# A graph layer's edge words sorted over four partitions at a time, for two batches at once, and 40 instead of 30 of 50 tiles read by one-hots

## The reference

```
h = relu(layernorm(x))
x = x + segment_sum((h * node_vec1)[src], dst) * node_vec1_n2
h = relu(layernorm(x))
x = x + (1 + eps) * h + segment_sum(relu(h[src] + edge_attr), dst)
```

## Time and profile before

| what | value |
|---|---|
| time, median of 3 runs (us) | 4988.89 (4985.14 to 4989.31) |
| the profiled execution's span (us) | 8580.9 |
| PE, DVE, ACT, POOL busy in it (us) | 4359, 3658, 3125, 3610 |
| indirect DMAs of POOL: scatters, gathers of layer two, gathers of middle tiles, of the last batch | 1875, 1250, 480, 50 |

### The profile page before, as it was taken

The page is one execution under the profiler, slowest core; times in us unless marked ns, Lnnn a source line. Parts: engine busy times, 40 slices in busy tenths (PEclk is TensorE's granted clock), DMA queues, the critical chain, the costliest instruction groups (busy, mean ns, idle before and its releaser), DMA issues.

```text
span 8580.9 us, 129759 instructions
## 1 busy us (share of the span) xinstructions
PE 4359.2 (51%) x44428; PEld 3164.9 (37%) x44428; DVE 3658.4 (43%) x11303; ACT 3124.7 (36%) x8299; POOL 3610.0 (42%) x3712
## 2 busy tenths in 40 slices
PE   0555555555555555555555555445444444545444
PEld 0333333333333333333333333334334343434343
DVE  6444444444444444444444444434343333434334
ACT  0333434343333333333333333234333333433333
POOL 7444444444444444444444444343443434343442
PEclk8777777777777777777777777666666666666666
DMA  5111111111111111111111100101110111101110
GB/s 90 31 31 31 31 31 31 31 30 31 30 31 30 31 30 31 30 31 30 31 30 31 31 17 17 43 22 31 30 32 22 32 29 32 31 22 32 30 32 17
DMA packets 437255, 265.45 MB, mean 31 GB/s; under 512 B 330740, under 2 KB 421220, under 8 KB 430120
## 3 DMA queue, kind: packets, MB, share of 16 engines
q1 hardware_dynamic: 318264, 185.91, 9.1%
q0 software_dynamic: 116960, 65.42, 4.4%
q10 hardware_dynamic: 1296, 4.79, 0.2%
HBM read 176.35 MB, written 79.52 MB: 30 GB/s over the span
## 4 chain that ended last, share of the span: by engine, by line
PE 36%; issue 26%; another core or an unknown queue 22%; DVE 9%; ACT 5%; SPq 1%; DVEq 0%; ACTq 0%; DMA 0%; POOL 0%; POOLq 0%
PE candidates L1179 16%; DVE arena L1663 5%; PE candidates L1105 5%; PE plain_ps L1191 4%; PE sorted_agg L1122 4%; DVE arena L1639 3%; PE key_rows L1074 2%; ACT centered L974 2%; PE candidates L1100 2%; ACT message L920 2%; PE plain_ps L1143 1%; PE candidates L1092 1%; ACT arena L821 1%; PE plain_ps L1151 1%
## 5 line engine op out<-in xcount | busy, mean ns | idle before, releaser
L710 POOL DMA_INDIRECT records<-stage,place_i x1875 | 1821.1, 971 | 675.8 <-issue 625.1
L698 POOL DMA_INDIRECT stage<-table,src_plain x1250 | 1193.9, 955 | 1778.1 <-DMA stage<-in_edge_attr 1386.7
L1639 DVE TENSOR_SCALAR arena<-arena,row_key 125x1280 bf16<-125x1280 f16 x1000 | 552.6, 553 | 2554.9 <-ACT arena L821 1776.0
L920 ACT ACTIVATE message<-candidates,member_is 128x96 bf16<-128x96 f32 x3600 | 912.4, 352 | 1643.5 <-remote 922.8
L691 POOL DMA_INDIRECT message<-table,mid_src x480 | 533.5, 1112 | 2234.8 <-PE plain_ps L1151 2095.5
L1105 PE MATMUL candidates<-parts,arena 125*128 125x32 bf16 x15000 | 589.2, 181 | 1214.2 <-issue 1211.8
L821 ACT ACTIVATE arena<-key_rows 125x640 f16<-125x640 f16 x1000 | 662.5, 719 | 1237.3 <-remote 987.2
L1663 DVE TENSOR_SCALAR arena<-window_iota,dst_rel 128x224 bf16<-128x224 f16 (+1 forms) x4800 | 1025.9, 280 | 112.4 <-remote 67.7
L1105 PEld LDWEIGHTS candidates<-parts,arena 125*128 125x128 bf16 x15000 | 503.7, 99 | 1384.6 <-issue 1370.1
L1092 PE MATMUL candidates<-parts,arena 125*128 125x96 bf16 x5000 | 312.0, 220 | 1312.9 <-ACT message L920 748.6
L1074 PE MATMUL key_rows<-ident,record 128*125 128x128 f16 x5000 | 494.6, 242 | 878.4 <-issue 587.7
(11 more groups left out here) (224 smaller groups left out, 5798.9 us busy)
## 6 DMA issues: line engine op xcount, KB each, us to landing
record<-records SPq DMA_DIRECT2D x50, 1650.0 KB, 7.1
stage<-in_edge_attr SPq DMA_DIRECT2D x125, 400.0 KB, 3.2
records<-pad SPq DMA_DIRECT2D x25, 1650.0 KB, 10.7
records<-stage,place_i POOLq DMA_INDIRECT x1875
stage<-table,src_plain POOLq DMA_INDIRECT x1250
message<-table,mid_src POOLq DMA_INDIRECT x480
xs<-in_x SPq DMA_DIRECT2D x8, 390.6 KB
table<-parts ACTq DMA_DIRECT2D x4, 585.9 KB
```

The source lines that it names most:

```text
L698: pool.indirect_dma_start(message[:, k, j, :] if l == 0 else rows[:, k, j, :], None, table0 if l == 0 else table1, bass.IndirectOffsetOnAx ...
L710: pool.indirect_dma_start(records, bass.IndirectOffsetOnAxis(ap=place_i[:, h, e:e + 1], axis=0), stage[:, h, e, :], None).then_inc(scatter ...
L920: last = nc.scalar.activation(direct_message[n % DB][:, m * WIDE:(m + 1) * WIDE], candidates[n % 2][:, m * WIDE:(m + 1) * WIDE], ACT.Copy, ...
L1639: nc.vector.tensor_scalar(src_onehot[:, g % 2, o, :], key_row[:, g % 2, :], row_key[0:NP, o:o + 1], None, ALU.is_equal).then_inc(src_oneho ...
```

## The change

The words of layer one are stored to DRAM once and come back as 64 rows of 200: four neighbouring partitions share a row (32 rows a batch), and two batches are sorted at the same time, in 25 rounds of MAX8 and MATCH_REPLACE8 over 200 words. Word 4k+j of the sorted row goes to tile k of the j-th of the four partitions, by a store to DRAM and a load. As 200 words are drawn instead of 50, a tile at a given rank meets fewer groups: the table `SPANS` gives 3 to 8. 20 tiles at either end are now read by one-hots, in eight steps of five instead of six, and 10 are gathered. The rounds of the sort stand in the main part of DVE's list, two to a group in groups 1 to 6 (12 rounds in an even batch, 13 and six closing passes in an odd one), the first pair's ahead of the first batch. SP issues the three transfers of a pair, ACT those of the first.

```diff
-    BOUNDS = (6, 7, 8, 8, 9, 9, 10, 10, 11, 11, 12, 12, 13, 13, 14)
-    SIDE = len(BOUNDS)
+    SPANS = ((0, 3), (0, 3), (0, 4), (0, 5), (0, 5), (0, 6), (0, 6), (0, 7), (1, 7), (1, 8),
+             (1, 8), (1, 9), (2, 9), (2, 10), (2, 10), (3, 10), (3, 11), (3, 11), (4, 12), (4, 12))
+    SIDE = 20
...
-        return range(BOUNDS[r]) if side == LOW else range(WIDES - BOUNDS[r], WIDES)
+        least, beyond = SPANS[r]
+        return range(least, beyond) if side == LOW else range(WIDES - beyond, WIDES - least)
...
+                if sorts_ahead(b) and h == 0:
+                    sp.wait_ge(words_out, 16 * (u + 1))
+                    sp.dma_start(pair_left, words_rows[bass.ds((b + 2) * QUADS, 2 * QUADS), :]).then_inc(pair_loaded, 16)
+                if sorts_ahead(b) and h == 1:
+                    sp.wait_ge(pair_steps, PAIR_STEPS * (u + 1))
+                    sp.dma_start(ordered_rows[bass.ds((b + 1) * QUADS, 2 * QUADS), :], pair_left).then_inc(words_out, 16)
+                    sp.wait_ge(words_out, 16 * (u + 2))
+                    sp.dma_start(row_words, ordered_v[:, bass.ds(b + 1, 2), :]).then_inc(words_loaded, 16)
...
+                if l == 0:
+                    act.wait_ge(direct_keyed, 1)
+                    act.dma_start(words_v, row_order[:]).then_inc(words_out, 16)
+                    act.wait_ge(words_out, 16)
+                    act.dma_start(pair_left, words_rows[0:2 * QUADS, :]).then_inc(pair_loaded, 16)
+                    act.wait_ge(pair_steps, PAIR_STEPS)
+                    act.dma_start(ordered_rows[0:2 * QUADS, :], pair_left).then_inc(words_out, 16)
+                    act.wait_ge(words_out, 32)
+                    act.dma_start(row_words, ordered_v[:, 0:2, :]).then_inc(words_loaded, 16)
...
+            def sort_pair(u, some):
...
+                for r in some:
+                    eight = pair_best[:, 8 * r:8 * r + 8]
+                    step(nc.vector.max(out=eight, in_=pair_left))
+                    if r < ROUNDS8 - 1:
+                        step(nc.vector.match_replace(out=pair_left, in_to_replace=eight, in_values=pair_left, imm_value=-1.0))
...
+                step(nc.vector.tensor_scalar(pair_left.rearrange("p (k e) -> p e k", k=SHARED), by_tile, pair_flag, None, ALU.add))
...
-            sort_rows(0, 0)
+            sort_pair(0, range(ROUNDS8))
+            dve.wait_ge(words_loaded, 16)
+            read_words(0, 0)
...
+                SORTING = [{g: range(2 * g - 2, 2 * g) for g in range(1, 7)}, {g: range(2 * g + 10, 2 * g + 12) for g in range(1, 7)}]
+                SORTING[1][7] = range(24, ROUNDS8)
...
                         if g == 4 and not is_first(b):
                             add_pair(b - 1)
+                        if sorts_ahead(b) and g in SORTING[h]:
+                            sort_pair(u, SORTING[h][g])
...
-                            sort_rows(b + 1, 1 - h)
...
+                            if s == SUBS - 4 and more:
+                                dve.wait_ge(words_loaded, 16 * (u + h))
+                                read_words(b + 1, 1 - h)
```

More of the change, by code:

```diff
@@ L80, in gnn_two_layers @@
     MID = PJ - DIRECTS
-    STEPS = ((LOW, range(4, -1, -1), "far"), (LOW, range(14, 9, -1), "arena"), (LOW, range(9, 4, -1), "near"),
-             (HIGH, range(14, 9, -1), "arena"), (HIGH, range(4, -1, -1), "far"), (HIGH, range(9, 4, -1), "near"))
-    SUBS = len(STEPS)
     SUB = 5
+    SIDE_STEPS = SIDE // SUB
+    SUBS = 2 * SIDE_STEPS
+    ROOMS = [("far", "arena", "near")[k % 3] for k in range(SUBS - 2)] + ["far", "near"]
+    STEPS = [(LOW, range(k * SUB, (k + 1) * SUB), ROOMS[k]) for k in range(SIDE_STEPS)]
+    STEPS += [(HIGH, range(SIDE - 1 - k * SUB, SIDE - 1 - (k + 1) * SUB, -1), ROOMS[SIDE_STEPS + k]) for k in range(SIDE_STEPS)]
+    LAST_ARENA = max(k for k in range(SUBS) if ROOMS[k] == "arena")
     TILE_OF = [(side, r) for side, ranks, _ in STEPS for r in ranks]
@@ L262, in gnn_two_layers @@
         wide_rooms += [record[0:NP, 1, :, :].rearrange("p t w -> p (t w)").bitcast(BF16)[:, w * SE5:(w + 1) * SE5] for w in range(IN_X)]
-        NEAR = BOUNDS[9]
-        assert NEAR + BOUNDS[4] <= len(wide_rooms)
+        NEAR = IN_X
+        assert all(len(STEP_GROUPS[k]) <= IN_X for k in range(SUBS) if ROOMS[k] != "arena")
         def wide_onehot(k, w):
@@ L288, in gnn_two_layers @@
         dst_far = sb("dst_far", [P, J], I32)
-        far = sb("far", [P, J])
-        far_dst = sb("far_dst", [P, J])
-        far_key = sb("far_key", [P, J])
+        far, far_dst, far_key = (row_room[:, (6 + k) * P:(6 + k) * P + J] for k in range(3))
         BANK = 512
@@ L368, in gnn_two_layers @@
         nodes_ready = sem("nodes_ready")
-        xs_steps = sem("xs_steps")
         result_ready = sem("result_ready")
@@ L495, in any_beyond, with sorts_ahead @@
             return eng.value_load(any_far_i[0:1, 0:1], min_val=0, max_val=1)
+        def sorts_ahead(b):
+            return not isinstance(b, int) or b < 2 + 2 * ROUNDS
         def is_last(b):
@@ L680, in _ @@
                       allow_small_or_imprecise_dtypes=True).then_inc(consts_ready, 1)
-            for r in range(SIDE):
-                pool.memset(bound[:, LOW, SIDE - 1 - r:SIDE - r], float(BOUNDS[r] * P)).then_inc(bounds_ready, 1)
-                pool.memset(bound[:, HIGH, r:r + 1], float((WIDES - BOUNDS[r]) * P)).then_inc(bounds_ready, 1)
+            GROUP_WORDS = P * LOWER
+            for q in range(PJ):
+                groups = met_by(HIGH, q) if q < SIDE else met_by(LOW, PJ - 1 - q) if q >= PJ - SIDE else range(WIDES)
+                pool.memset(least_word[:, q:q + 1], float(groups.start * GROUP_WORDS)).then_inc(bounds_ready, 1)
+                pool.memset(beyond_word[:, q:q + 1], float(groups.stop * GROUP_WORDS)).then_inc(bounds_ready, 1)
             pool.iota(members[:], pattern=[[1, MEMBERS]], base=0, channel_multiplier=0,
@@ L1706, in wide_onehots @@
                     dve.wait_ge(direct_copied_keys, SUBS * b + s + 1)
-                    if s == 1:
+                    held = [k for k in range(s) if ROOMS[k] == where]
+                    if held:
+                        dve.wait_ge(wide_picked, DIRECTS * b + FIRST[held[-1] + 1])
+                    elif where == "arena":
                         dve.wait_ge(sorted_done[0], GROUPS * (b + 1))
-                    elif s == 3:
-                        dve.wait_ge(wide_picked, DIRECTS * b + FIRST[2])
-                    elif s >= 4:
-                        dve.wait_ge(wide_picked, DIRECTS * b + FIRST[s - 3])
                     else:
```

138 lines of the change are left out of this document (82 added, 56 removed).

## The result

| | before | changed |
|---|---|---|
| time, median (us) | 4987.02 (4983.14 to 4989.31, 4 runs) | 5182.28 (5173.41 to 5202.59, 4 runs) |
| the profiled execution's span (us) | 8580.9 | 5171.3 |

The changed kernel is slower by 3.95%: a ratio of 1.0395, with a 95% interval of 1.0372 to 1.0418. Its recording is not stretched as that of before was: its span is that of a timed run (5171.3 of 5173.41 us), so stretches can be read from it directly.

What follows compares the result with a forecast made beforehand. POOL's DMAs bound the kernel before (125.6 us a batch); the changed PE/DVE/ACT loop, 117.1 - 1.1 + 14.5 = 130.5, replaces them. First middle products 260.5, batches 3233, then 52.5, 52.9, 55, 1652 and 61: 5105 us, range 4860 to 5300.

Steps and rivals of the forecast that it cites:

- What bounds before: Layer one: POOL's 95 DMAs bound a batch at 125.6 us; PE's loop with DVE and ACT takes 117.1, 8.5 to spare.
- What ten gathers fewer buy: POOL in 24 batches: 85 DMAs, 112.4 us a batch, 13.2 less; it buys only the distance to the next bound.
- The sort: DVE's main part: rounds of 1.10 us, groups of 5.3 instead of 3.12, all on the path: +14.5 us a batch.
- loop 117.1 - 1.1: PE's loop of 117.1 us a batch less 1.1 in the direct part: 116 in batches without a sort.
- 81.8 - 1.6 - 5.3: Direct part on PE: 81.8 us before, 1.6 of waiting in its last steps, net -5.3 of PE work by the change.
- 1652 + 61 of the sum: End of the kernel: layer two's 1250 gathers 1652 us, then 61 from the last gather to the end.
- The price of 1.322 us a DMA: POOL's indirect DMAs: 4608 us of the timed run for 3485 DMAs, if POOL is the bound throughout.
- The rule of the Trainium skill: POOL in busier main parts: lockout with DVE could make DMAs as slow as 1.54 us, 130.9 a batch.
- POOL stays the bound: Rival: PE and DVE's loop is below 125.5 us, change faster, 4820 at 10%; faster by either way 0.25.
- The loop is longer still: Rival: PE's loop before was near 125 us, sort on top, up to 5290, or 5370 with 2.02 us rounds; chance 0.19.
- The sort is hidden: Rival: DVE, idle for half of the span, hides the sort, giving 4800; faster by either way 0.25.
- the 5015 for a sort that does not grow: Rival case: sort time grows with no word, 11 us a pair-half instead of 14.5, giving 5015.

## Why the prediction held, and where it was off

The prediction (5105, within 4860 to 5300, slower) held: 5182.28 lies in the range, and slower is what it is. Of the 195 us that the change costs it had 116.

*What bounds before.* Right. POOL issues without a pause, 126.9 us a batch (125.6 in the prediction), and PE waits for records. The spare time of PE's loop, 8.5 us in the prediction, is 8.1 by the rows above. That the difference comes out is in part luck: both loops are longer than priced, POOL's by 1.3 us and the other (118.9 against 117.1) by 1.8.

*What ten gathers fewer buy.* Right in kind: the distance to the next bound, 183 us in the run that leaves only them out.

*The sort.* Right in place and size. Rounds of 1.08 us (1.10), 5.34 us a group (5.3), PE waiting for destination one-hots, and 135.06 - 120.8 = 14.3 us a batch where 14.5 was expected. The rival by which it is hidden in DVE's idle half fails for this placement; put into the direct part, the same rounds cost 121.8 - 120.8 = 1 us a batch.

*The mis-sized term* is "loop 117.1 - 1.1", the 116 us of a batch without the sort: 35.3 of main and 80.7 of direct part. It is 120.8. The two batches shown above of the run without the later sorts have 242.4 us where the prediction has 232, and the 10.4 lie in three places. The loop's jump, 3.5 us in the two, which the prediction did not have: in the kernel before it lies under PE's wait for POOL. The direct part, 1.0 longer in each: PE is busy for 76.2 us of it, where the prediction's prices leave 74.9 (81.8 - 1.6 - 5.3), a walk over tiles that left out small work on PE. And the main part, 2.5 longer in each even without the jump. That POOL scatters during it, which it did not do in the stretch that 35.3 was read from the earlier trace rows, is not the reason: in the kernel before with ten gathers fewer a main part with 28 scatters in it takes 34.25 us. That main part, its first matmuls up to the second set of picks, and the same 50 matmuls at the start of the main part of 37.80 us:

```profile
1950.79:1985.04 34.25, 27.72 (x418) 26.29 (x419) 31.15 (x115) 27.23 (x56) 26.02 (x28) 1.00 0.07 15
1950.79:1954.14 3.35, 3.35 (x50) 3.35 (x51) 3.09 (x14) 1.39 (x4) 2.44 (x4) 1.00 0.05 10
```

```profile
794.50 1.78 PE L1143 MATMUL candidates<-parts,arena 125*128 125x96 bf16 x20 [2.39 <-ACT message L971]
```

```profile
794.50:800.41 5.91, 5.91 (x50) 5.91 (x51) 5.54 (x22) 1.49 (x4) 4.58 (x5) 0.55 0.07 14
```

With a wait of 1.36 us for ACT ahead of them they ran at a granted clock of 1.00; with one of 2.39 us at 0.55, mostly the lower of its two levels (1.2 GHz), and took 2.56 us longer. That is most of the 3.55 us between these two main parts. The stretch of 35.3 us itself began slowly, behind a long wait (its first picks took 1.78 us, the 50 matmuls 5.16), so against it the start explains 0.75 of the 2.5; the rest stays open.

*Two errors that partly cancel.* Times 21 batches the loop was 96 us too short, and the first pick came at 187.4 instead of 180.6, mainly because the store of the words took 10.1 us instead of 4. Against that, layer two took 5171.3 - 3497.9 = 1673 us from its first gather, 40 less than the 1652 + 61 of the sum: 30 less up to the last gather and 10 less behind it. Together, 96 + 7 - 40 = 63 of the 65 us by which the 5171.3 of this execution lie above the 5106. The price of 1.322 us a DMA was one mean over both layers, where it is 1.34 in layer one of the kernel before (above) and 1622 / 1249 = 1.30 in layer two, by the line's own row in the changed kernel (durations in ns, first and last start):

```profile
L740 POOL DMA_INDIRECT stage<-table,src_plain x1250: 940/944/3151, 3497.9 to 5119.9; - x179
```

*The rule of the Trainium skill.* The Trainium skill (SBUF — State Buffer, "Who interferes with whom") says that GpSimd and a VectorE operation in a two-port mode lock each other out; from that the prediction allowed for 1.54 us a DMA in the busier main parts. The stretch of 52.49 us above has 41 DMAs, 1.28 each, with DVE busy for 44.87 us of it: here the rows do not show that slowing, and the 1.54 of the first scatter is not a price for the rest. The trace of the kernel before could have said so: at the end of that scatter, while DVE runs the rounds over 50 words, the DMAs that start from 135.47 to 139.26 are 1.26 us apart, the undisturbed pitch. So "DVE at work" is too wide a condition; which of its operations slow POOL was not tested.

*The rivals.* "POOL stays the bound" fails on POOL's waits of 21 us. "The loop is longer still" named the right term and a larger size: PE's loop before is not near 125 but 118.9, as the run with ten gathers fewer shows. "The sort is hidden" fails as said above. One slip in their sums: the 5015 for a sort that does not grow takes 3.9 us a batch where 14.5 - 11 is 3.5, which gives 5023; nothing else hangs on it.

## What to carry to other kernels

Work taken off the engine that sets the pace is worth no more than the distance to the next engine's loop: measure that distance first, by leaving the work out. A helper's work is priced by the place it is put: the same rounds cost 14.3 us a batch in the part where DVE led and PE waited for it, and 1 in the part where DVE had 18 to 20 us idle. And when one bound is lifted, price what lay hidden under it (here the loop's jump, and a start of the main part at a lower clock), which no row of the old chain shows.

## What the hardware showed unexpectedly

The same kernel's recording took 8580.9 us once and 4983.4 us another time, at the same timed median. A jump back of the loop over batches lengthens the batch by some 3.3 us when nothing hides it (3.3 to 5.1 in the runs here). Behind waits of 2.65 to 7.76 us PE ran ten products in 1.47 to 2.07 us and the twenty picks after them in 1.8, where behind waits of 0.83 to 1.18 us they took 1.13 and 1.02; the granted clock of a main part with such waits was 0.80 on the mean, 0.95 without. The same 50 matmuls at the start of a main part took 3.35 us at a granted clock of 1.00 and 5.91 at 0.55, behind waits of 1.36 and 2.39 us.
